# Score products of two query tiles on half the rows each: a decoder layer in one kernel

## The reference, cut to what matters

```
q = rope((x @ Wq.T).reshape(B, L, 32, 64)); k = rope((x @ Wk.T).reshape(B, L, 8, 64))
attn = einsum('bkgqd,bkld->bkgql', qh, kh) * 64 ** -0.5      # causal
p = softmax(attn); out = einsum('bkgql,bkld->bkgqd', p, vh)
x = layernorm(x + out @ Wo.T)
x = layernorm(x + smooth_quant_linear(x, fside, ctx))
x = layernorm(x + (relu((x @ sign(up).T) * up_scale) @ sign(down).T) * down_scale * output_scale)
```

## Time and profile before

| | |
|---|---|
| median of 3 runs | 1481.37 us (1480.9 to 1482.57) |
| the profiled execution, its own time | 1484.37 us |
| its span | 1482.6 us |
| mean granted PE clock, as a share of full speed | 0.974 |
| PE busy | 1313.8 us, 89% of the span |
| DVE, ACT, POOL busy | 998.1, 940.2, 751.6 us |
| score products (three widths) | 1024, of 7099 on PE |
| DMAs from `q_tmp` to `q_st` | 512 of 64 KB |

### The profile page before, as it was taken

The page is one execution under the profiler, slowest core; times in us unless marked ns, Lnnn a source line. Parts: engine busy times, 40 slices in busy tenths (PEclk is TensorE's granted clock), DMA queues, the critical chain, the costliest instruction groups (busy, mean ns, idle before and its releaser), DMA issues.

```text
span 1482.6 us, 25047 instructions
## 1 busy us (share of the span) xinstructions
PE 1313.8 (89%) x7099; PEld 1081.3 (73%) x7112; DVE 998.1 (67%) x2435; ACT 940.2 (63%) x2197; POOL 751.6 (51%) x641
## 2 busy tenths in 40 slices
PE   3799999999999999898889888878897889899996
PEld 2588888888888877677777777767776667677775
DVE  3467777767777767878776786778777676744222
ACT  2576677676777776676767766666776584644332
POOL 3456555556556665465535464556441263536343
PEclk9799999999999999999999999999999999999999
DMA  4422212222122233222122222221235311010000
GB/s 170 147 75 65 58 50 67 64 78 60 50 61 58 72 89 100 72 64 58 50 62 76 58 51 58 79 57 47 52 86 162 139 37 49 18 40 3 26 29 28
DMA packets 54852, 98.78 MB, mean 67 GB/s; under 512 B 11744, under 2 KB 13792, under 8 KB 53728
## 3 DMA queue, kind: packets, MB, share of 16 engines
q1 hardware_dynamic: 54752, 97.57, 23.3%
HBM read 51.39 MB, written 4.19 MB: 37 GB/s over the span
## 4 chain that ended last, share of the span: by engine, by line
PE 63%; DVE 14%; ACT 10%; issue 7%; POOL 4%; DMA 1%; ACTq 0%; DVEq 0%; POOLq 0%; SPq 0%
PE m L1588 26%; PE ps_s L1588 8%; PE ps_o L1645 6%; PE ps_t L1633 6%; PE m L1873 6%; PE ps_s L1887 3%; PE ps_t L1887 3%; ACT pT_hi L1028 2%; DVE pT_lo L1308 2%; PE m L1655 2%; ACT probs L1020 2%; DVE o_sum L1261 1%; DVE probs L1247 1%; POOL y L963 1%; DVE sm_a L1361 1%
## 5 line engine op out<-in xcount | busy, mean ns | idle before, releaser
L1020 ACT ACTIVATE probs<-probs,neg_max 128x128 f32<-128x128 f32 (+3 forms) x512 | 285.2, 559 | 179.0 <-DVE neg_max L1247 178.4
L1308 DVE TENSOR_TENSOR pT_lo<-ps_t,pT_hi 128x512 fp32r<-128x512 f32 (+1 forms) x384 | 220.7, 595 | 148.0 <-ACT pT_hi L1028 145.8
L1633 PE MATMUL ps_t<-ident,probs 128*128 128x128 f32 x1280 | 188.3, 278 | 91.8 <-DVE pT_lo L1308 76.3
L1588 PE MATMUL ps_s<-k_st,q_st 128*128 128x256 f32 (+2 forms) x1024 | 236.0, 354 | 0.3 <-DVE neg_max L1247 0.3
L1633 PEld LDWEIGHTS ps_t<-ident,probs 128*128 128x128 f32 x1280 | 146.3, 142 | 122.4 <-DVE pT_lo L1308 94.8
L1247 DVE CUSTOM_DVE_ANT_0 probs<-ps_s,mask 128x128 f32<-128x128 f32 (+3 forms) x512 | 228.1, 482 | 6.8 <-PE ps_s L1588 6.6
L881 POOL TENSOR_TENSOR o_lo<-o_sum,o_hi 128x512 fp32r<-128x512 f32 x64 | 82.7, 1293 | 252.1 <-ACT o_hi L1042 252.1
L1028 ACT ACTIVATE pT_hi<-ps_t 128x512 fp32r<-128x512 f32 (+1 forms) x384 | 185.7, 518 | 5.6 <-PE ps_t L1633 2.5
L934 POOL TENSOR_TENSOR hid_lo<-hid,hid_hi 128x512 fp32r<-128x512 f32 x64 | 83.9, 1313 | 166.2 <-ACT hid_hi L1212 166.1
L1645 PE MATMUL ps_o<-pT_hi,v_st 128*128 128x256 f32 (+2 forms) x512 | 167.8, 339 | 0.0
L1588 PEld LDWEIGHTS ps_s<-k_st,q_st 128*128 128x128 f32 x1024 | 154.0, 195 | 4.0 <-DVE neg_max L1247 0.5
(11 more groups left out here) (251 smaller groups left out, 3064.9 us busy)
## 6 DMA issues: line engine op xcount, KB each, us to landing
q_st<-q_tmp SPq DMA_DIRECT2D x512, 64.0 KB, 2.0
raw<-in_wq_t SPq DMA_DIRECT2D x32, 256.0 KB, 3.0
k_st<-k_st SPq DMA_DIRECT2D x64, 128.0 KB, 2.4
raw<-in_wo_t SPq DMA_DIRECT2D x32, 256.0 KB, 3.0
raw_b<-in_ffn_t SPq DMA_DIRECT2D x10, 512.0 KB, 7.5
y<-in_x_t SPq DMA_DIRECT2D x4, 1024.0 KB, 10.8
raw<-in_wkv_t SPq DMA_DIRECT2D x16, 256.0 KB, 3.7
y<-in_x SPq DMA_DIRECT2D x4, 1024.0 KB, 5.7
```

The source lines that it names most:

```text
L1020: act.activation(probs[:, h % 2, SO[i]:SO[i] + SW[i]], probs[:, h % 2, SO[i]:SO[i] + SW[i]], ACT.Exp, bias=neg_max[:, h % 2, i:i + 1], sca ...
L1308: dve.tensor_tensor(pT_lo[:, d, :], ps_t[:, (h + k) % 2, 0:P * w].rearrange("p (w c) -> p w c", c=P), f32(pT_hi[:, d, :]), ALU.subtract).t ...
L1588: i = pe.matmul(dst, a, c, start=(j == 0), stop=(j == len(terms) - 1))
L1633: i = pe.transpose(ps_t[:, (h + k) % 2, P * c:P * (c + 1)], probs[:, h % 2, at:at + P], ident[:, :])
```

## The change

The second product of a score tile leaves out the low part of q. It takes 64 rows alone, the high part of q with the low part of k. For even tiles these are rows 0 to 63, for odd tiles rows 64 to 127; so for odd query tiles the parts in `q_st` change places (low parts on partitions 0 to 63, high parts on 64 to 127). k's parts lie on both halves and stay. The scores are made for two tiles at a time: first both products over 128 rows, then both products over 64 rows, one on either half of the rows and each to its own bank.

To put even and odd tiles on different partitions, each DMA of `move_q` becomes two, each with two pieces of 512 bytes on 32 partitions (32 KB): 32 DMAs for a unit. Their order is by head (`EARLY + LATE`), and each head has a semaphore of its own, for which PE waits before that head's scores. DVE's `rope_q` "even" waits for all four. In the first unit, k's parts are moved between `EARLY` and `LATE`.

```
             def move_q(u):
-                for k, t in enumerate((1, 3, 0, 2)):
...
-                    for h in range(G - 1):
-                        wait(sp, scored, u * (4 * G) - (4 * G - 4 * h - 4))
-                        sp.dma_start(f32(q_st[HF * k:HF * (k + 1), h, :]),
-                                     q_tmp[HF * h:HF * (h + 1), t, :]).then_inc(q_moved, 16)
-                for h in (G - 1,):
-                    wait(sp, scored, u * (4 * G))
-                    for k, t in enumerate((1, 3, 0, 2)):
-                        sp.dma_start(...).then_inc(q_moved_last, 16)
+            EARLY = ((0, (0, 1)), (1, (0, 1)), (0, (2, 3)), (1, (2, 3)))
+            LATE = ((2, (0, 1, 2, 3)), (3, (0, 1, 2, 3)))
+            def move_q(u, parts):
+                for h, ks in parts:
+                    wait(sp, scored, u * (4 * G) - (4 * G - 4 * h - 4))
+                    for k in ks:
+                        if k < 2:
+                            sp.wait_ge(q_hi, u * 2 + (k + 1))
+                        else:
+                            sp.wait_ge(q_lo, u * 2 + (k - 1))
+                        to = q_st[:, h, :].rearrange("p (t e c) -> p e t c", e=2, c=P)
+                        of = q_tmp[HF * h:HF * (h + 1), (1, 3, 0, 2)[k], :].rearrange("p (t e c) -> p e t c", e=2, c=P)
+                        for e in range(2):
+                            at = HF * ((k + 2 * e) % 4)
+                            sp.dma_start(f32(to[at:at + HF, e, :, :]), of[:, e, :, :]).then_inc(q_moved[h], 16)
...
-            move_q(0)
+            move_q(0, EARLY)
             move_k(0, 0)
+            move_q(0, LATE)
...
-                        move_q(u + 1)
+                        move_q(u + 1, EARLY + LATE)
...
             def rope_q(fill, u, what):
                 if what == "even":
-                    wait(dve, q_moved, u * (16 * 4 * (G - 1)))
-                    wait(dve, q_moved_last, u * (16 * 4))
+                    for moved in q_moved:
+                        wait(dve, moved, u * (16 * 8))
...
-            def scores(n, u, h, buf, i):
...
-                wait(pe, maxed, n * 4 + (i - 1))
-                w = max(2 * P, SW[i])
-                product(ps_s[:, i % 2, 0:w], [(q_st[:, h, P * i:P * (i + 1)], k_st[:, buf, s, 0:w]) for s in range(2)]
-                        ).then_inc(scored, 1)
+            def scores(n, u, h, buf, j):
+                if j == 0:
+                    if h == 0:
+                        pe.wait_ge(k_dup, (u + 1) * 32)
+                    pe.wait_ge(q_moved[h], (u + 1) * (16 * 8))
+                tiles = (2 * j, 2 * j + 1)
+                for i in tiles:
+                    wait(pe, maxed, n * 4 + (i - 1))
+                    w = max(2 * P, SW[i])
+                    pe.matmul(ps_s[:, i % 2, 0:w], q_st[:, h, P * i:P * (i + 1)], k_st[:, buf, 0, 0:w], start=True, stop=False)
+                for i in tiles:
+                    w = max(2 * P, SW[i])
+                    e = slice(HD * (i % 2), HD * (i % 2) + HD)
+                    pe.matmul(ps_s[:, i % 2, 0:w], q_st[e, h, P * i:P * (i + 1)], k_st[e, buf, 1, 0:w],
+                              start=False, stop=True).then_inc(scored, 1)
```

More of the change, by code:

```diff
@@ L438, in build @@
         q_lo = sem("q_lo")
-        q_moved = sem("q_moved")
-        q_moved_last = sem("q_moved_last")
+        q_moved = [sem(f"q_moved{h}") for h in range(G)]
         v_hi = sem("v_hi")
@@ L692, in move_k @@
                 sp.dma_start(f32(k_st[HD:P, buf, 1, :]), f32(k_st[0:HD, buf, 1, :])).then_inc(k_dup, 16)
-            def move_q(u):
-                for k, t in enumerate((1, 3, 0, 2)):
[L697 to L700, removed]
-                    for h in range(G - 1):
-                        wait(sp, scored, u * (4 * G) - (4 * G - 4 * h - 4))
-                        sp.dma_start(f32(q_st[HF * k:HF * (k + 1), h, :]),
-                                     q_tmp[HF * h:HF * (h + 1), t, :]).then_inc(q_moved, 16)
-                for h in (G - 1,):
-                    wait(sp, scored, u * (4 * G))
-                    for k, t in enumerate((1, 3, 0, 2)):
-                        sp.dma_start(f32(q_st[HF * k:HF * (k + 1), h, :]),
-                                     q_tmp[HF * h:HF * (h + 1), t, :]).then_inc(q_moved_last, 16)
-            move_q(0)
+            EARLY = ((0, (0, 1)), (1, (0, 1)), (0, (2, 3)), (1, (2, 3)))
[14 more added lines that the diff above has]
+            move_q(0, EARLY)
             move_k(0, 0)
+            move_q(0, LATE)
             load_x(0)
@@ L758, in load_tile @@
                 elif h == 4:
-                    sp.wait_ge(q_moved, U * (16 * 4 * (G - 1)))
-                    sp.wait_ge(q_moved_last, U * (16 * 4))
+                    for moved in q_moved:
+                        sp.wait_ge(moved, U * (16 * 8))
                 elif h == 6:
@@ L1677, in _ @@
             pe.wait_ge(consts, 4)
-            for i in range(QT):
-                scores(0, 0, 0, 0, i)
+            for j in range(2):
+                scores(0, 0, 0, 0, j)
             project(len(M0_BEFORE), 1, "even")
@@ L1697, in body @@
                             scores(*ahead, 0)
-                            scores(*ahead, 1)
                         if h == 0 and b != 1 and prev:
@@ L1704, in body @@
                         if more:
-                            scores(*ahead, 2)
-                            scores(*ahead, 3)
+                            scores(*ahead, 1)
                         if half == 1:
```

## The result

The changed kernel takes 1618.93 us (median of 4 runs, 1616.32 to 1620.83) against 1481.97 us before (1480.9 to 1482.87): a ratio of 1.0923, 95% interval 1.0904 to 1.0942, slower by 137 us. The forecast was 1590 us, slower by 109, with a range of 1515 to 1640. The profiled execution took 1616.32 us with a span of 1614.5; its mean granted clock is 0.942 (0.974 before).

The account below looks back on a forecast made before the run. PE's work was taken to bound the kernel, with anything delaying DVE before `pT_lo`. Later ropes 54, weights 8, products 33 and clock 14 us made 109 us over 1481.4: 1590 us, range 1515 to 1640.

Parts of the forecast that it names:

- The bound and its mechanism: PE's work bounds the kernel; 16 more issues on SP delay DVE's rope, then `pT_lo`, then PE: 54 us.
- Price of an issue: On SP's queue, each split move of q takes 0.63 us to issue, so 16 more add 10.1 us a unit.
- Net 2.4 and 2.7 us, so 2.55 us a unit: PE's delay behind DVE's late rope, after idle time absorbs some; 15 first-half units: 38 us.
- k's and v's are issued at 236.88 and land 3.7 us later: Weights queued behind the moves come 4.9 us late, ACT stalls about 2 us every second unit: 8 us, bounds 0 and 32.
- 33 us: Score products on PE: 0.30 us more a pair, 27 us behind the rope plus 6 us in later units.
- Three pairs lie between the rope and the next moves: In each of 30 units, three of eight score pairs count fully at 0.30 us each: 27 us.
- I count 8 of 30: Eight of 30 PE stalls are followed by half clock, 1.7 us each: 14 us, bounds 0 and 51.
- (b): Issues at or below 0.50 us on SP's queue, nobody waits, products overlap at no cost: 1456 us; chance 0.07.
- (c): Cheap issues on SP's queue, but switching rows on PE costs 51 us: 1532 us; chance 0.08.
- (e): Cheap issues on SP's queue; cost and gain of PE's score products cancel: 1481 us; chance 0.04.
- (a): SP's queue makes DVE late, but PE's narrow products overlap and switching is free: 1544 us; chance 0.20.
- (d): 0.5 us a score pair, every PE stall lowers the clock, weights at their upper bound: 1663 us; chance 0.12.

Follow-up runs that it names:

- 24 moves: Kernel before with the new by-head order and semaphores, old scores, heads 0 and 1 moved whole, only heads 2 and 3 in split moves: 1486.52 us.
- work in PE's stall: Changed kernel plus five or eight unread 512-column products on PE at h = 0, in the first eight steps but one: 1605.07 us.
- after: The changed kernel itself, with 32 moves a unit and the 64-row second products, against the kernel before: 1618.93 us.
- The version with 32 moves and nobody behind them: Changed kernel with low parts moved earlier, `rope_q` "even" awaiting only those, q, k, v weights before the moves, Wo's after the first eight: 1524.85 us.

## Why the prediction was right, and where it was off

**The bound and its mechanism: right.** Sixteen more issues on SP's queue make DVE late for its rope, DVE's `pT_lo` is late behind it, and PE waits. SP's share of the chain, DVE's 28 waits for a DMA and the fall to 1486.52 us with 24 moves show it. The threshold was put at 17.6 us of queue and landing; 24 moves reach it and cost 5 us. Three signs came out a little beside their marks: DVE's wait is 4.3 us (2 to 4 forecast), PE's wait for `pT_lo` 114 us (over 120), a unit 37.5 us (about 35). One reading of the rows was wrong without effect: head 0 needs twelve issues at 0.63 us as before, so it is complete no earlier.

**Price of an issue: right, slightly low.** 0.63 us was taken and 0.655 measured. The DMA with half the bytes in two pieces is not cheaper. The last one lands 22.4 us after the first issue, not 21.6: 0.8 us in each unit that binds.

**The stall in steady units: undersized.** The step that failed is "Net 2.4 and 2.7 us, so 2.55 us a unit", which let idle time behind the rope absorb part of the delay. The rope comes 4.9 us (22.50 for 17.60) and 5.2 us (22.37 for 17.15) later, where 4.0 and 4.5 were forecast, and none of it is absorbed: from the rope to the next moves the two units take 14.70 and 15.24 us (the second from 283.49 to 298.73), where they took 14.55 and 14.25 (243.04 to 257.29). In the mean of thirteen units the rope is 5.2 us later and the stretch behind it 0.6 us longer, together the 5.8.

What took the place of the idle time? Not the three pairs of scores that lie there: with the same moves and the old scores the two units take 14.34 and 15.59 us (245.14 to 259.48, 281.97 to 297.56), as much in sum. With work in PE's stall, and so without half clock, they take 13.16 and 14.40 (275.88 to 290.28), in sum 2.4 us less than after and 1.2 less than before. So some absorption exists, 0.6 us a unit where 1.6 and 1.8 were forecast, and the half clock behind the stall takes it away. ACT's wait for Wo's weights (2.10 us) lies in the same stretch; its share wasn't separated.

With the prediction's own terms for the weights, the clock and three pairs (0.5, 0.5 and 0.9 us) a steady unit was to be 4.4 us longer; it is 5.8. Over thirteen units this is 18 of the 28 us that the sum lacks. In the later fifteen the terms make about 2.9 a unit and 2.7 was measured.

**The weights: named, but undersized and not complete.** The step is "k's and v's are issued at 236.88 and land 3.7 us later", with 8 us, and 32 as its upper bound. Wo's two loads, which stand behind the moves in the other kind of unit, have no term; ACT waits for them 28.7 us in after. In after removing one wait hardly shows, since DVE is late at the same time: taking away one kind of weights gives 5 us, taking away the rope's wait 19. With the rope's wait gone and the old scores, 109 us are left with both kinds of weights late, and with all three waits gone 3 us. The three waits cover each other: from 1619, removed one after another (the rope's, that for q's, k's and v's weights, that for Wo's), they give 19, 36 and 39 us.

**The products: sign and size right, their place wrong.** A pair costs 0.22 and 0.27 us net (0.30 forecast). The full overlap, which the sum assumed, is there, and it saves 0.14 (0.145). The Trainium skill's rule that a change of tiling mode drains TensorE (TensorEngine Tiling, Key Properties) agrees with PEld's idle time around the pairs shown, 0.31 and 0.24 us in the wide one and 0.13 us twice in the narrow one. The Trainium skill's promise of up to twice the speed (TensorEngine Tiling, Theoretical Speedup) agrees for the two 64-row products taken alone, and is outweighed by the two switches around them. But the term "33 us", on top of the stalls, was too large: alone the products cost 39 us, behind the late moves only 6. The step that failed is "Three pairs lie between the rope and the next moves", priced in full: units with the new and the old scores are equally long there, 37.5 us. The sum added two costs that lie side by side.

**The clock: too small.** 1.7 us for a stall is what the window at 250.40 shows (3.4 us at 0.51). The step "I count 8 of 30" is wrong: 12 stretches in the first half (85 to 620 us) were at half clock after, against 1 before, and from 620 to 1250 us it was 78.5 us of such time against 41.0. These windows end before the attention of after does. By the mean granted clocks, 0.942 of 1614.5 us and 0.974 of 1482.6, the whole executions have 187 and 77 us at half clock: 110 us more, 55 us of PE's work lost. By the work put in the stall, where 14 of 22 us came back, I estimate the term at 35 us instead of 14. That share is measured in the first half alone; for the rest it is an assumption.

**The sum.** 28 us short of 137. The stalls and the clock were each too small, the products too large. That the total fell inside the range owes something to these errors having both signs.

**Rivals.** Cheap issues, rivals (b), (c) and (e), are ruled out by 0.655 us. Switching for free, rival (a), is ruled out by 0.22 and 0.27 us a pair. The heavy case (d), 1663 us, had two of its parts: nearly every stall of the first half lowers the clock, and the weights matter; but a pair doesn't cost 0.5 us.

**What stays open.** The version with 32 moves and nobody behind them is slower than before, by 2.8%. No kernel run here beats the one before by more than the noise. Changing the parts' places within `q_tmp`, so that 16 whole DMAs would do, was not tried, nor were the moves on another engine's queue. As the products alone cost 39 us, I expect that neither would bring the change much under that; no run shows it. Pairs that share one switch to 64 rows, all four tiles of a head, were not tried either; it needs four banks for the scores at a time, where the kernel has two.

## What to carry to other kernels

A queue that issues DMAs is filled by issues, not bytes (0.33 to 0.655 us each here, the largest DMA the cheapest), and extra ones are nearly free (5 us for eight more a unit here) until the first waiter behind them comes later than its slack; so list everything that stands behind them (buffer reuse, each kind of weights), since removing one wait only uncovers the next. Running two half-height products side by side pays only if what the overlap saves exceeds the switch to half the rows and back; here it saved 0.14 us against 0.385. And don't add the cost of more work on an engine to the cost of stalls on the same engine: price each alone, then ask which of them covers the other.

## What was not expected of the hardware

- Two products on separate halves of the rows start 2 to 4 ns apart (all 256 pairs) and overlap completely, their weight loads too (0.19 us for both).
- A move of 32 KB in pieces of 512 bytes is issued at 0.655 us, one of 64 KB at 0.63 us, while a load of 256 KB takes 0.33 us of the same queue.
- In the first half of after, eight of nine idle stretches of PE of 2.4 to 3.3 us went with a fall to half clock, which then lasted 3.4 or 6.8 us. With work in the stall there was, up to 600 us, none after stretches of 1.2 to 1.5 us, one each after 1.65 and 1.71 us, and none after three of 2.4 to 2.8 us. So the length of the idle stretch alone doesn't decide it.
